# A soft mixture-of-experts block on one Trainium2 core: the softmax shifts of the first phase contract 64 rows in each half of the array instead of 128

## The reference, cut to what matters

```python
xn = _layernorm(x, axis=-1)
logits = (einsum('tzd,ed->tze', xn, phi_w) + phi_b).reshape(t, z, n, p)   # n = 64, p = 32
D = softmax(logits, axis=3)          # over the 32 slots of an expert
C = softmax(logits, axis=2)          # over the 64 experts of a slot
X_tilde = einsum('tznp,tzd->npd', D, xn)
...                                  # clip, normalise, tanh, expert weights -> Y_tilde
Y = einsum('tznp,npH->tzH', C, Y_tilde)
```

## Time and profile before

| | us |
|---|---|
| median of 3 runs | 1187.13 (1187.02 to 1187.49) |
| span of the profiled execution | 1184.2 |
| what lies around the span, against the median | 2.9 |
| PE busy | 1144.7 (97%), 5097 matmuls |
| DVE busy | 1050.1 (89%) |
| ACT busy | 981.7 (83%) |
| POOL busy | 958.9 (81%) |
| granted clock of TensorE, mean | 0.998 of 2.4 GHz |

### The profile page before, as it was taken

One profiled execution on the slowest core, in us unless ns is written; L12 is line 12 of the kernel. 1 busy time (PEld: TensorE's weight loads), 2 busy tenths in 40 slices (PEclk: granted clock), 3 DMA queues, 4 the chain that ended last, 5 costly groups with the idle time before them and its releaser, 6 DMA issues. The chain is left out here.

```text
span 1184.2 us, 17639 instructions
## 1 busy us (share of the span) xinstructions
PE 1144.7 (97%) x5097; PEld 787.9 (67%) x5097; DVE 1050.1 (89%) x1608; ACT 981.7 (83%) x2128; POOL 958.9 (81%) x770
## 2 busy tenths in 40 slices
PE   5999999999999999999989999999999999999996
PEld 3666666565666666666457777777777777777764
DVE  7999999999999999999767888888888888888887
ACT  5877877877766766766668999999999999999998
POOL 3998999898999999999788777878777788877751
PEclk9999999999999999999999999999999999999999
DMA  4445435434424432443754444344444444444420
GB/s 131 152 152 200 141 140 182 153 128 164 155 109 160 155 133 113 161 156 129 225 188 154 131 142 143 119 147 128 142 143 143 131 128 134 141 128 142 142 72 18
DMA packets 125263, 167.36 MB, mean 141 GB/s; under 512 B 7536, under 2 KB 102000, under 8 KB 125040
## 3 DMA queue, kind: packets, MB, share of 16 engines
q1 hardware_dynamic: 123984, 165.71, 41.4%
q10 hardware_dynamic: 1184, 0.53, 0.2%
HBM read 90.71 MB, written 75.50 MB: 140 GB/s over the span
## 5 line engine op out<-in xcount | busy, mean ns | idle before, releaser
L146 POOL TENSOR_TENSOR exp_slots_loaded<-exp_slots_loaded,slot_max 128x1024 f32<-128x1024 f32 x128 | 323.2, 2545 | 6.6 <-DMA exp_slots_loaded<-exp_slots 3.2
L858 POOL TENSOR_TENSOR dd<-ed,rz 128x512 f32<-128x512 f32 x256 | 267.6, 1051 | 24.7 <-ACT rz L688 23.4
L563 PE MATMUL acc<-dd,xns 128*128 128x512 f32 x512 | 261.1, 592 | 0.7 <-POOL dd L858 0.7
L1917 DVE TENSOR_TENSOR clo<-ct,chi 128x512 fp32r<-128x512 f32 x256 | 171.5, 681 | 24.3 <-ACT chi L1585 21.6
L176 POOL TENSOR_TENSOR ch<-exp_slots_loaded 128x512 f32<-128x512 f32 x128 | 165.9, 1296 | 32.0 <-ACT exp_slots_loaded L666 30.9
L795 DVE TENSOR_REDUCE mr<-lg 128x16 fp32r<-128x512 f32 x256 | 168.0, 685 | 19.3 <-PE lg L506 16.9
L657 ACT ACTIVATE ed<-lg 128x512 f32<-128x512 f32 x256 | 145.6, 594 | 40.3 <-PE lg L540 38.4
L666 ACT ACTIVATE exp_slots_loaded<-lg 128x512 f32<-128x512 f32 x256 | 145.5, 594 | 26.4 <-PE lg L549 24.4
L1585 ACT ACTIVATE chi<-ct 128x512 fp32r<-128x512 f32 x256 | 147.7, 597 | 11.8 <-PE ct L1219 8.3
L1219 PE MATMUL ct<-identity,exp_slots_loaded 128*128 128x128 f32 x1024 | 150.9, 273 | 5.6 <-POOL exp_slots_loaded L146 3.1
L811 DVE TENSOR_REDUCE zd<-ed 128x32 f32<-128x1024 f32 x128 | 154.6, 1208 | 1.5 <-ACT ed L657 1.5
(11 more groups left out here) (315 smaller groups left out, 2500.2 us busy)
## 6 DMA issues: line engine op xcount, KB each, us to landing
exp_slots<-exp_slots_loaded SPq DMA_DIRECT2D x128, 512.0 KB, 3.4
exp_slots_loaded<-exp_slots SPq DMA_DIRECT2D x128, 512.0 KB, 3.5
xns<-xn_rows SPq DMA_DIRECT2D x128, 64.0 KB, 1.9
b_xraw<-in_xT SPq DMA_DIRECT2D x16, 256.0 KB, 3.8
out_t<-b_ti SPq DMA_DIRECT2D x15, 256.0 KB, 2.1
expert_w_late<-in_expert_w SPq DMA_DIRECT2D x5, 512.0 KB, 11.1
xn_rows<-slot_sum SPq DMA_DIRECT2D x8, 256.0 KB, 2.5
expert_w_early<-in_expert_w SPq DMA_DIRECT2D x3, 512.0 KB, 5.8
```

The lines of the kernel that those rows point to most:

```text
L146: e.tensor_tensor(rows, rows, joined(SM, b)[:, h].unsqueeze(2).broadcast_to([P, TPB, GC * EPC, NP]), ALU.mult).then_inc(s_we)
L563: e.matmul(acc[k][:, :], xns[v % RX][:, :], dd[v % RX][:, bank(k)], start=tile == 0, stop=tile == NT - 1, skip_group_check=True).then_inc( ...
L858: e.tensor_tensor(dd[v % RX][:, bank(k)].rearrange("q (n p) -> q n p", p=NP), ed[v % RD][:, bank(k)].rearrange("q (n p) -> q n p", p=NP), ...
L1917: e.tensor_tensor(clo[g % RC][:, :], ct[c % 2][:, :], hi_f32(chi[g % RC][:, :]), ALU.subtract).then_inc(c_l)
```

## The change

- `mr` has 64 columns instead of 128, and the zeros and the semaphore for them go.
- `turn_max` makes two plain fp32 products of the 64 columns with the identity instead of one transpose: one puts the 64 rows in rows 0 to 63 of `tr`, the other puts the same rows in 64 to 127.
- `S1M` and `S2M` are 128x512. Rows 0 to 63 hold the pattern of bank 0, rows 64 to 127 that of bank 1. `shift_experts(k)` and `shift_slots(k)` contract the rows 64k to 64k + 63 alone.
- In TensorE's order both banks of `shift_experts` now always stand together, and both of `shift_slots` too; an `x_tilde` or `tiles_turned` that stood between them goes ahead of the pair or behind it.
- The patterns are made by six `affine_select` of 32x512 instead of three of 32x1024. The fills and copies of them have half the columns.

```diff
-        S1M = sb(front, "shift_experts", [P, HS], F32R)
-        S2M = sb(front, "shift_experts_to_slots", [P, HS], F32R)
+        S1M = sb(front, "shift_experts", [P, BANK], F32R)
+        S2M = sb(front, "shift_experts_to_slots", [P, BANK], F32R)
...
-            mr = [sb(ph, f"mr{b}", [P, P], F32R) for b in range(2)]
+            mr = [sb(ph, f"mr{b}", [P, G], F32R) for b in range(2)]
...
+            def rows_of(k):
+                return slice(k * G, (k + 1) * G)
...
-                for b in range(2):
-                    e.memset(hi_f32(mr[b][:, G:P]), 0.0).then_inc(s_zero)
...
-                pattern(1, shifts[0][0:32, :].rearrange("r (n p) -> r n p", p=NP), -1.0, [[-1, HN], [0, NP]])
-                pattern(2, shifts[1][0:32, :].rearrange("r (n p) -> r n p", p=NP), 1.0, [[-1, HN], [0, NP]])
-                pattern(3, shifts[1][HN:HN + 32, :].rearrange("r (n p) -> r n p", p=NP), -1.0, [[0, HN], [-1, NP]])
+                for k in range(2):
+                    pattern(1 + k, pattern_rows(0, k * G), -1.0, [[-1, HN // 2], [0, NP]], -k * HN // 2)
+                for k in range(2):
+                    pattern(3 + 2 * k, pattern_rows(1, k * G), 1.0, [[-1, HN // 2], [0, NP]], -k * HN // 2)
+                    pattern(4 + 2 * k, pattern_rows(1, k * G + HN), -1.0, [[0, HN // 2], [-1, NP]])
...
                 def turn_max(i, r):
...
-                        if v < 2:
-                            e.wait_ge(s_zero, v + 1)
-                        e.transpose(tr[v % 2], hi_f32(mr[v % 2][:, :]), IDENT[:, :]).then_inc(s_tr)
+                        for k in range(2):
+                            done = e.matmul(tr[v % 2][rows_of(k), :], hi_f32(mr[v % 2][:, :]), IDENT[:, :], start=True, stop=True)
+                        done.then_inc(s_tr)
...
-                        e.matmul(lg[v % 2][:, bank(k)], mt[v % 2][:, :], S1M[:, bank(k)], start=False, stop=True,
+                        e.matmul(lg[v % 2][:, bank(k)], mt[v % 2][rows_of(k), :], S1M[rows_of(k), :], start=False, stop=True,
...
-                        e.matmul(lg[v % 2][:, bank(k)], mt[v % 2][:, :], S2M[:, bank(k)], start=False, stop=True,
+                        e.matmul(lg[v % 2][:, bank(k)], mt[v % 2][rows_of(k), :], S2M[rows_of(k), :], start=False, stop=True,
...
                 for i in range(-3, UNITS // TPB + 3):
+                    shift_experts(i - 2, 2, 0)
+                    shift_experts(i - 2, 2, 1)
                     logits(i - 2, 3, 1)
-                    shift_experts(i - 2, 2, 1)
...
                     x_tilde(i - 2, 1, 0)
+                    x_tilde(i - 2, 1, 1)
                     shift_slots(i - 2, 3, 0)
-                    x_tilde(i - 2, 1, 1)
                     shift_slots(i - 2, 3, 1)
...
+                    x_tilde(i - 2, 2, 0)
                     shift_slots(i - 1, 0, 0)
-                    x_tilde(i - 2, 2, 0)
                     shift_slots(i - 1, 0, 1)
...
+                    tiles_turned(i - 1)
                     shift_slots(i - 1, 1, 0)
-                    tiles_turned(i - 1)
                     shift_slots(i - 1, 1, 1)
...
-                    shift_experts(i - 1, 2, 0)
```

More of the change, by code:

```diff
@@ L262, in build @@
             phi_second = XTT[:, HS:2 * HS].rearrange("q (c d) -> q c d", d=P)
-            shifts = dd[1:3]
+            shifts = [dd[b][:, 0:BANK] for b in (1, 2)]
+            def rows_of(k):
+                return slice(k * G, (k + 1) * G)
             HC = CH // 2
@@ L375, in scalar0 @@
                 e.wait_ge(s_id, PATTERNS)
-                e.activation(S1M[:, :], shifts[0][:, :], ACT.Copy).then_inc(s_sc)
-                e.activation(S2M[:, :], shifts[1][:, :], ACT.Copy).then_inc(s_sc)
+                e.activation(S1M[:, :], shifts[0], ACT.Copy).then_inc(s_sc)
+                e.activation(S2M[:, :], shifts[1], ACT.Copy).then_inc(s_sc)
             def vector0(e):
                 for k in range(2):
-                    e.memset(shifts[k][:, :], 0.0).then_inc(s_id)
+                    e.memset(shifts[k], 0.0).then_inc(s_id)
                 for k, value in enumerate((1e-5, 1e-6, 1e-8, 0.0, 1.0)):
@@ L417, in gpsimd0, with pattern, pattern_rows @@
                 e.memset(IDENT[:, :], 0.0).then_inc(s_id)
-                def pattern(nth, dst, fill, step):
+                def pattern(nth, dst, fill, step, base=0):
                     e.wait_ge(s_id, 3 + nth)
-                    e.affine_select(out=dst, in_=dst, compare_op=ALU.not_equal, fill=fill, base=0, pattern=step,
+                    e.affine_select(out=dst, in_=dst, compare_op=ALU.not_equal, fill=fill, base=base, pattern=step,
                                     channel_multiplier=1).then_inc(s_id)
+                def pattern_rows(shift, first):
+                    return shifts[shift][first:first + 32, :].rearrange("r (n p) -> r n p", p=NP)
                 pattern(0, IDENT[:, :], 1.0, [[-1, P]])
-                pattern(1, shifts[0][0:32, :].rearrange("r (n p) -> r n p", p=NP), -1.0, [[-1, HN], [0, NP]])
-                pattern(2, shifts[1][0:32, :].rearrange("r (n p) -> r n p", p=NP), 1.0, [[-1, HN], [0, NP]])
-                pattern(3, shifts[1][HN:HN + 32, :].rearrange("r (n p) -> r n p", p=NP), -1.0, [[0, HN], [-1, NP]])
+                for k in range(2):
[3 more added lines that the diff above has]
+                    pattern(4 + 2 * k, pattern_rows(1, k * G + HN), -1.0, [[0, HN // 2], [-1, NP]])
                 e.wait_ge(s_id, PATTERNS)
```

3 lines of the change are left out of this document (1 added, 2 removed).

## The result

The changed kernel takes 1276.79 us (median of 4 runs, 1273.45 to 1279.07) against 1187.18 before (4 runs too): a ratio of 1.0754, 95% interval 1.0742 to 1.0767. It is 90 us slower; forecast were 88.

A forecast was written before the change was run, and what follows sets the result against it. DVE was taken to bound the first phase early, PE later. PE at 4.96 us per unit (5.05 in the first half) loses 0.71 x 79 = 56 plus 0.65 x 49 = 32: +88 us, 1275, range 1190 to 1335.

The forecast's parts named there:

- The bound: First phase: DVE bounds the first regime (60 to 240 us), PE the second (300 to 540 us), 4.14 of 4.25 us per unit.
- Shifts side by side: Shift matmuls of a pair stream together: two pairs take 0.48 instead of 0.92 us per unit, a gain of 0.44.
- Rival 3: Pairs split by rows run one after the other: 59 us more, 1334 us; chance 0.07.
- The two products: Turning the maxima by two plain fp32 products takes 0.22 instead of 0.12 us per unit, a loss of 0.10.
- The start: Making and copying the patterns at the kernel's start: zero effect, both ways.
- The price of a change: Tile size changes on PE: 0.22 us returning, 0.22 into 64 rows, 0.17 into 64 columns; 1.16 per unit.
- No waits: PE's time per unit in the first phase: no waits added to 4.96 us, since DVE (4.04) and POOL (4.00) run ahead.
- moving `x_tilde` ahead of `shift_slots` costs no time of the array: TensorE's new order in the first phase: no array time lost, second shifts mostly finding their exponentials done.
- The sum of 4.96: PE time per unit in us: 1.38 + 1.72 + 0.48 + 0.22 + 1.16; 5.05 in the first half.
- Rivals 1 and 2: First: size changes cost nothing, 1170 us, chance 0.14. Second: half the price, 1205, up to 1225, chance 0.20.
- Rival 2's upper number: Half-price case's upper time: up to 1225 us if today's 0.11 us of waits per unit stays.
- DVE idle for 15 to 20% in both regimes: Expected sign in the changed kernel's first phase: DVE idle some 15 to 20% of the time, waiting for the logits.

The follow-up runs named there:

- rows without overlap: Kernel before, with both shifts contracting rows 0 to 63 only, same order, so nothing can overlap: 1310.07 us, ratio 1.1058.
- 128*128 product: Kernel before, with the transpose of the maxima replaced by one plain fp32 product of 128 columns with the identity: 1198.95 us, ratio 1.0101.
- Products alone: Kernel before, with only the transpose of the maxima replaced by two plain products of 64 columns: 1234.54 us, ratio 1.0403.
- pairs only: Changed kernel, but maxima turned by one transpose as before and ACT copying the 64 rows twice: 1245.87 us, ratio 1.0498.

## Why the prediction was right, point by point

- **The bound** was read rightly. TensorE carries the second regime, and the first has so little room (4.14 + 0.09 of array time under a period of 4.40) that it turns over as well.
- **Shifts side by side**: taken from a split by columns, and right for one by rows. 0.227 of a possible 0.231 is saved (rows without overlap against the changed kernel). Rival 3 falls.
- **The two products**: 0.22 as forecast. The 128*128 product confirms it from outside: 12 us, forecast 9.
- **The start**: nothing, as forecast. POOL's six patterns end at 7.58 us, and it still waits for DVE until 8.49.

```profile
2.60 4.98 POOL L421 TENSOR_SCALAR_AFFINE_SELECT dd<-dd 32x512 f32<-32x512 f32 x6
8.49 1.04 POOL L435 TENSOR_TENSOR dd<-dd,bias 128x512 f32<-128x512 f32 x1 [0.91 <-DVE bias L328]
```

- **The price of a change**: forecast 0.22, 0.22 and 0.17, from one place in the second phase; measured 0.20 out, 0.19 to 0.20 into 64 rows, 0.14 into 64 columns. Per iteration 10 x 0.20 + 8 x 0.195 + 4 x 0.14 = 4.12 instead of 4.64, so 1.03 per unit instead of 1.16. The term was 0.13 too large.
- **No waits** was wrong by as much in the other direction. By its own terms a unit is 3.80 + 1.03 = 4.83; the trace has 4.98 to 5.00. The 0.15 are waits. At one place in each iteration the logits wait for `exp_slots` after the turn (next lines), and at one the second shift of a pair waits 0.18 for its exponentials. The first costs 0.38: the turn's stream ends at 447.27, the load could have started at 447.38 and did at 447.76.

```profile
447.00 0.44 PE L536 MATMUL tr<-identity,mr 128*64 128x128 f32 x4
447.76 0.50 PE L509 MATMUL lg<-phi_then_expert_out,xn_transposed 128*128 128x512 f32 x1 [0.32 <-ACT exp_slots_loaded L671]
```

  The sentence "moving `x_tilde` ahead of `shift_slots` costs no time of the array" is true and beside the point: it costs time on the way to the next logits, which I had not followed. The sum of 4.96 against 4.98 rests on these two errors, equal and opposite: that 88 came so near to 90 is luck, and the price alone would have given some 17 us less. In the first stretch it is alike (5.05 against 5.11). The mechanism and the total are right; two terms are not.
- **Rivals 1 and 2** fall. In the lines on the weight loads above, every load across a change starts about 0.1 us after the stream of the other size has ended, never during it. (Rival 2's upper number should be 1219: today's waits of 0.11 are 14 us over 128 units, on top of 1205.) The Trainium skill, TensorEngine Tiling (Array Packing), section Tiling Modes, has the rule that held here, a change of mode drains the array. The Trainium skill, TensorE: Matmul & The Clock Gate, in its step-by-step part, tells of weight loads that are pulled ahead of running matmuls. The trace has this within one size only: L510's load starts at 443.44, 0.23 ahead of its matmul, while L509 streams.
- **DVE idle for 15 to 20% in both regimes**: 17.5% in the second, 10.5% in the first, where DVE also has the statistics to make; I had not counted them there.

The effects add up only roughly. Products alone cost 48 us and pairs alone 59, together 107; the changed kernel pays 90. Twice per iteration a pair and a turn are neighbours and save one change out, 2 x 0.20 x 32 = 13 us. The rest may be the waits, which are shorter than in pairs only (0.38 and 0.18 against some 0.70 and 0.36); that isn't parted further.

## What to carry to other kernels

Before splitting the array for small matmuls between full-sized ones, count the visits, not the matmuls: here each visit to another size cost 0.35 to 0.39 us, and two matmuls of 512 columns side by side give back 0.23. It takes more work for one visit (an estimate from these figures: two packed pairs in one visit would gain 0.46 and win; it wasn't tried), or a phase that stays in one size. And when a call is moved in a hand-written order, follow what reuses its buffer two units later: the changed order alone cost 20 us without any change of operands, 15 of them by one call.

## What was not expected of the hardware

- A direct step from 64 rows to 64 columns costs 0.144 us, the same as from 128*128 to 64 columns (0.142 to 0.144). In the steps that occur here, what is paid depends on the size entered, not on the one left: 0.14 for 64 weight columns and 0.19 to 0.20 for 128, whether of 64 or of 128 rows. The difference of 0.05 is what 64 columns fewer to load would save (an estimate: a load of 128 columns in the open took 0.11). A step from 64 columns to 64 rows doesn't occur.
- A split by rows overlaps as completely as one by columns: two 64*128 matmuls of 512 columns start 2 to 4 ns apart and take the time of one, when neither waits.
